# A gated cross-attention and mixture-of-experts kernel: first stage with two kv buffers, squares and the statistics of x on ScalarE, and the gate one block later

## What is computed

```python
kv = einsum('bhil,bhjl->bijhl', k, v)               # k = v = context, 8 x 8 products a head
y = irfft(rfft(kv, 2 * L) * rfft(ssm_kernel, 2 * L))[..., :L]
out = einsum('bijhl,bhil->bjhl', y + kv * D, q)     # q = layernorm(x)
x = x + tanh(g_xattn) * out
t = layernorm(x)
x = x + tanh(g_ffn) * (routed_experts(t) + shared_expert(t))
```

## Time and profile before

| | |
|---|---|
| median of three runs | 766.82 us (766.34 to 770.25) |
| the profiled execution | 769.46 us, span 767.5 us |
| PE busy | 725.1 us, 94% of the span |
| PEld busy | 675.8 us, 88% |
| DVE busy | 577.8 us, 75% |
| ACT busy | 431.1 us, 56% |
| POOL busy | 381.5 us, 50% |
| DMA | 114.32 MB, mean 149 GB/s |

### The profile page before, as it was taken

How to read it: one execution, slowest core, us unless ns; L and a number is a source line. 1 busy time by engine, 2 the same in 40 slices (tenths; PEclk the granted TensorE clock), 3 DMA queues, 4 the chain that set the end, 5 groups by cost and what they waited for, 6 DMA issues and landing times.

```text
span 767.5 us, 15537 instructions
## 1 busy us (share of the span) xinstructions
PE 725.1 (94%) x4602; PEld 675.8 (88%) x4602; DVE 577.8 (75%) x1152; ACT 431.1 (56%) x579; POOL 381.5 (50%) x191
## 2 busy tenths in 40 slices
PE   2899999999999999999999999999999999999993
PEld 2889899989888999999998999889899989999992
DVE  5889898999975469433799588679758985895892
ACT  3444444444432322123789577668758875895882
POOL 2898989888800137021335443344343435544242
PEclk9999999999999999999999999999999999999998
DMA  6658677776522211263466577677646575434200
GB/s 194 224 188 246 226 238 236 229 246 218 207 96 70 56 28 42 42 242 74 129 173 178 116 256 182 176 188 197 176 112 179 139 210 149 94 73 72 42 16 0
DMA packets 47425, 114.32 MB, mean 149 GB/s; under 512 B 7392, under 2 KB 7392, under 8 KB 47360
## 3 DMA queue, kind: packets, MB, share of 16 engines
q1 hardware_dynamic: 34528, 88.62, 34.8%
q0 software_dynamic: 12832, 24.93, 17.3%
HBM read 157.25 MB, written 29.26 MB: 243 GB/s over the span
## 4 chain that ended last, share of the span: by engine, by line
PE 58%; DVE 16%; DMA 8%; issue 7%; ACT 5%; SPq 2%; ACTq 1%; DVEq 1%; POOL 0%; POOLq 0%
PE pair L1196 15%; PE bank L1196 12%; PE pair L1221 10%; PE bank L1221 5%; PE pair L1132 5%; DMA out<-ys,slot_info 4%; DMA raw<-in_weights 3%; PE bank L1090 3%; PE bank L1143 3%; PE pair L1204 2%; DVE st L693 2%; DVE prod L746 2%; DVE bank L751 2%; DVE rows L758 2%; ACT xn L550 2%
## 5 line engine op out<-in xcount | busy, mean ns | idle before, releaser
L1063 DVE TENSOR_TENSOR w_lo<-raw,w_hi 128x1408 fp32r<-128x1408 f32 x94 | 148.8, 1622 | 44.8 <-ACT w_hi L650 44.8
L1319 POOL DMA_INDIRECT tn<-t_rows,slot_info x47 | 71.2, 1516 | 134.1 <-DVE tT_lo L803 117.6
L1330 POOL DMA_INDIRECT out<-ys,slot_info x47 | 86.3, 1836 | 100.3 <-DMA out<-ys,slot_info 70.6
L650 ACT ACTIVATE w_hi<-raw 128x1408 fp32r x94 | 124.9, 1375 | 5.9 <-DMA raw<-in_weights 3.8
L1132 PE MATMUL pair<-kv_hi,toep_hi 128*128 128x288 f32 x320 | 100.5, 314 | 4.4 <-issue 1.9
L1068 DVE TENSOR_TENSOR w_lo<-raw,w_hi 128x1536 fp32r<-128x1536 f32 x47 | 82.4, 1754 | 17.4 <-ACT w_hi L657 17.2
L1132 PE MATMUL pair<-kv_hi,toep_lo 128*128 128x288 f32 x320 | 95.3, 298 | 0.0
L1132 PE MATMUL pair<-kv_lo,toep_hi 128*128 128x288 f32 x320 | 95.1, 297 | 0.0
L1275 POOL TENSOR_TENSOR kv_lo<-kv,kv_hi 128x2304 fp32r<-128x2304 f32 (+1 forms) x16 | 79.6, 4972 | 18.8 <-ACT kv_hi L582 18.8
L657 ACT ACTIVATE w_hi<-raw 128x1536 fp32r x47 | 69.4, 1477 | 15.5 <-DMA raw<-in_weights 15.4
L1330 POOL DMA_INDIRECT out<-ys,own_row x16 | 27.4, 1713 | 82.5 <-ACT ys L638 76.1
(11 more groups left out here) (213 smaller groups left out, 2012.6 us busy)
## 6 DMA issues: line engine op xcount, KB each, us to landing
raw<-in_weights SPq DMA_DIRECT2D x94, 704.0 KB
raw<-in_weights SPq DMA_DIRECT2D x47, 768.0 KB
toep_hi<-kpad_hi SPq DMA_DIRECT2D x16, 512.0 KB, 4.1
toep_lo<-kpad_lo SPq DMA_DIRECT2D x16, 512.0 KB, 6.0
cx<-in_ctx SPq DMA_DIRECT2D x16, 384.0 KB, 6.3
stage<-in_weights SPq DMA_DIRECT2D x16, 272.0 KB, 4.5
xt<-in_x SPq DMA_DIRECT2D x16, 256.0 KB, 6.4
xr<-in_x SPq DMA_DIRECT2D x16, 256.0 KB, 6.5
```

The source lines that it names most:

```text
L650: act.activation(w_hi[s % 2][:, a:b], raw[:, bass.ds(half + a, b - a)], ACT.Copy).then_inc(hi_ok[n_], 1)
L1063: dve.tensor_tensor(w_lo[s % 2][:, a:b], raw[:, bass.ds(half + a, b - a)], w_hi[s % 2][:, a:b].bitcast(F32), ALU.subtract).then_inc(lo_ok[ ...
L1319: pool.indirect_dma_start(out=tn[o % 2][:], out_offset=None, in_=t_rows, in_offset=bass.IndirectOffsetOnAxis(ap=slot_info[:, 3 * i:3 * i + ...
L1330: pool.indirect_dma_start(out=out, out_offset=bass.IndirectOffsetOnAxis(ap=rows, axis=0), in_=ys[o % 2][:], in_offset=None, bounds_check=R ...
```

## The change

`kv` gets a second buffer. `form` leaves out the squares (3 groups of pairs in place of 4 in its first operation), and POOL does it for tile `t+2` in turn `t`, still ahead of `split_shared(t)` and `split_kv(t+1)`; `form(1)` goes ahead of the first turn. The squares are written by a new `square(t)` on ACT, also two tiles ahead; `split_kv_hi` waits for it. The mean and variance of `x` come from ACT: a Copy with scale -1/L and a Square with the negated mean as bias, both with `accum_out`, and the full outputs go to a scratch tile `spent`. DVE's `stats_x` goes, and `scale_x(t+1)` moves ahead of `products(t,2)`. In ACT's turn `split_shared`, `split_kv_hi` and `std_x` go ahead of `std_x2`. SP loads `ctx` one tile earlier. PE does `gate(t-2)` behind `conv(t,1)` in place of behind `conv(t,0)`.

```diff
--- before.py
+++ after.py
@@ -202,16 +202,17 @@
...
-        st1, st2 = sb2("st1_", [P, 6], F32, one), sb2("st2_", [P, 6], F32, one)
+        st2 = sb2("st2_", [P, 6], F32, one)
         mv1, mv2 = sb2("mv1_", [P, 3], F32, one), sb2("mv2_", [P, 3], F32, one)
         sd1, sd2 = sb2("sd1_", [P, 2], F32, one), sb2("sd2_", [P, 2], F32, one)
-        kv = sb("kv", [P, BLOCKS * GROUPS * PAIRS], F32, one)
+        kv = sb2("kv", [P, BLOCKS * GROUPS * PAIRS], F32, one)
...
+        spent = sb("spent", [P, L], F32, one)
...
@@ -271,7 +272,7 @@
...
-        q_turned, q_ok, kv_ok = sem("q_turned"), sem("q_ok"), sem("kv_ok")
+        q_turned, q_ok, kv_ok, square_ok = sem("q_turned"), sem("q_ok"), sem("kv_ok"), sem("square_ok")
...
@@ -302,11 +303,12 @@
...
-            n = (TILES - 4) // 2
+            n = (TILES - 6) // 2
...
-            turn(At(TILES - 1))
+            for t in range(TILES - 3, TILES):
+                turn(At(t))
@@ -362,16 +364,16 @@
         def form(eng, t):
 
             p = t.odd
-            wait(eng, kvl2_ok, t)
-            if t.within(1, 2):
+            wait(eng, kvl2_ok, t - 1)
+            if t.within(2, 3):
                 eng.wait_ge(kvl_ok, 1)
             wait(eng, ctx_in[p], (t.half() + 1) * 16)
             g, hb = BLOCKS * 2, HD * BATCH
-            eng.tensor_tensor(view(kv[:], 0, [[PAIRS * BATCH, g], [hb, 4], [1, hb]]),
-                              view(cx[p][:], 0, [[EXT * BATCH, g], [0, 4], [1, hb]]),
-                              view(cx[p][:], 0, [[EXT * BATCH, g], [BATCH, 4], [1, hb]]),
+            eng.tensor_tensor(view(kv[p][:], hb, [[PAIRS * BATCH, g], [hb, 3], [1, hb]]),
+                              view(cx[p][:], 0, [[EXT * BATCH, g], [0, 3], [1, hb]]),
+                              view(cx[p][:], BATCH, [[EXT * BATCH, g], [BATCH, 3], [1, hb]]),
                               ALU.mult).then_inc(kv_ok, 1)
-            eng.tensor_tensor(view(kv[:], 4 * hb, [[PAIRS * BATCH, g], [1, hb // 2]]),
+            eng.tensor_tensor(view(kv[p][:], 4 * hb, [[PAIRS * BATCH, g], [1, hb // 2]]),
                               view(cx[p][:], 0, [[EXT * BATCH, g], [1, hb // 2]]),
                               view(cx[p][:], hb // 2, [[EXT * BATCH, g], [1, hb // 2]]),
                               ALU.mult).then_inc(kv_ok, 1)
@@ -429,6 +431,9 @@
             load(At(0), "toep")
             load(At(1), "ctx")
             load(At(1), "x")
+            sp.wait_ge(kv_ok, 2)
+            sp.wait_ge(square_ok, 1)
+            load(At(2), "ctx")
             load(At(1), "toep")
             sp.dma_start(gw[:], gate_w).then_inc(consts_in, 16)
...
@@ -444,9 +449,11 @@
 
             def turn(t):
                 first, ahead = t.within(0, 1), not t.within(TILES - 2, TILES)
+                if not t.within(TILES - 3, TILES):
+                    wait(sp, kv_ok, (t + 2) * 2)
+                    wait(sp, square_ok, t + 2)
+                    load(t + 3, "ctx")
                 if ahead:
-                    wait(sp, kv_ok, (t + 1) * 2)
-                    load(t + 2, "ctx")
                     wait(sp, xn_ok, t + 1)
                     load(t + 2, "x")
                 if not first:
@@ -536,8 +543,17 @@
             act.activation(small[:, 3:4], small[:, 0:1], ACT.Sqrt)
 
             def std_x(t):
+
+                p = t.odd
+                wait(act, x_in[p], (t.half() + 1) * 16)
+                wait(act, rstd1, (t - 1) * 2)
+                act.activation(spent[:], xt[p][:], ACT.Copy, scale=-1.0 / L, accum_out=mv1[p][:, 0:1]).then_inc(stat1, 1)
+                wait(act, stat1, t * 2 + 1)
+                act.activation(spent[:], xt[p][:], ACT.Square, bias=mv1[p][:, 0:1],
+                               accum_out=mv1[p][:, 1:2]).then_inc(stat1, 1)
                 wait(act, stat1, (t + 1) * 2)
-                act.activation(sd1[t.odd][:, 0:1], mv1[t.odd][:, 1:2], ACT.Sqrt, bias=small[:, 0:1]).then_inc(std1, 1)
+                act.activation(sd1[p][:, 0:1], mv1[p][:, 1:2], ACT.Sqrt, bias=small[:, 0:1],
+                               scale=1.0 / L).then_inc(std1, 1)
 
...
@@ -579,7 +595,19 @@
                 p = t.odd
                 wait(act, conv_ok, (t - 1) * 8)
                 wait(act, kv_ok, (t + 1) * 2)
-                act.activation(kv_hi[p][:], kv[:], ACT.Copy).then_inc(kvh_ok, 1)
+                wait(act, square_ok, t + 1)
+                act.activation(kv_hi[p][:], kv[p][:], ACT.Copy).then_inc(kvh_ok, 1)
+
+            def square(t):
+
+                p = t.odd
+                wait(act, kvl2_ok, t - 1)
+                if t.within(2, 3):
+                    act.wait_ge(kvl_ok, 1)
+                wait(act, ctx_in[p], (t.half() + 1) * 16)
+                g, hb = BLOCKS * 2, HD * BATCH
+                act.activation(view(kv[p][:], 0, [[PAIRS * BATCH, g], [1, hb]]),
+                               view(cx[p][:], 0, [[EXT * BATCH, g], [1, hb]]), ACT.Square).then_inc(square_ok, 1)
 
...
@@ -587,26 +615,31 @@
                 wait(act, stage_in[p], (t.half() + 1) * 16)
                 act.activation(shared_hi[:, bass.ds(t.v * STAGE, STAGE)], stage[p][:], ACT.Copy).then_inc(shi_ok, 1)
 
+            square(At(0))
             act.wait_ge(kpad_ok, 1)
             act.activation(krow_hi[:], krow[:], ACT.Copy).then_inc(krowh_ok, 1)
             split_kv_hi(At(0))
             std_x(At(0))
             norm_x(At(0))
             q_copy(At(0))
+            square(At(1))
 
             def turn(t):
-                if not t.within(0, 1):
+                first, last = t.within(0, 1), t.within(TILES - 1, TILES)
+                split_shared(t)
+                if not last:
+                    split_kv_hi(t + 1)
+                    std_x(t + 1)
+                if not first:
                     std_x2(t - 1)
-                split_shared(t)
-                if not t.within(TILES - 1, TILES):
-                    split_kv_hi(t + 1)
-                if not t.within(0, 1):
+                if not t.within(TILES - 2, TILES):
+                    square(t + 2)
+                if not first:
                     norm_x2(t - 1)
-                if not t.within(TILES - 1, TILES):
-                    std_x(t + 1)
+                if not last:
                     norm_x(t + 1)
                     q_copy(t + 1)
-                if not t.within(0, 1):
+                if not first:
                     tT_copy(t - 1)
 
             pairs(act, turn)
@@ -695,18 +728,14 @@
                 dve.tensor_copy(hop[:, 1:2], hop[:, 0:1])
                 dve.bn_aggr(mv[p][:, 0:2], st[p][:]).then_inc(ok, 1)
 
-            def stats_x(t):
-                wait(dve, x_in[t.odd], (t.half() + 1) * 16)
-                stats(xt, st1, mv1, stat1, t)
-
             def scale_x(t):
 
                 p = t.odd
                 wait(dve, std1, t + 1)
                 dve.reciprocal(sd1[p][:, 1:2], sd1[p][:, 0:1]).then_inc(rstd1, 1)
                 wait(dve, rstd1, t * 2 + 1)
-                dve.tensor_scalar(mv1[p][:, 2:3], mv1[p][:, 0:1], sd1[p][:, 1:2], -1.0,
-                                  ALU.mult, ALU.mult).then_inc(rstd1, 1)
+                dve.tensor_scalar(mv1[p][:, 2:3], mv1[p][:, 0:1], sd1[p][:, 1:2], None,
+                                  ALU.mult).then_inc(rstd1, 1)
 
...
@@ -769,7 +798,6 @@
             form(dve, At(0))
-            stats_x(At(0))
             dve.memset(prod[0][:], 0.0).then_inc(setup_dve, 1)
             scale_x(At(0))
             dve.memset(prod[1][:], 0.0).then_inc(setup_dve, 1)
@@ -788,10 +816,8 @@
                 if not first:
                     scale_x2(t - 1)
                 if not last:
-                    stats_x(t + 1)
+                    scale_x(t + 1)
                 products(t, 2)
-                if not last:
-                    scale_x(t + 1)
                 products(t, 3)
 
             pairs(dve, turn)
@@ -1149,11 +1175,11 @@
             def turn(t):
                 first, last = t.within(0, 1), t.within(TILES - 1, TILES)
                 conv(t, 0)
-                if not first and not t.within(1, 2):
-                    gate(t - 2)
                 if not first:
                     sum_rows(t - 1, 3)
                 conv(t, 1)
+                if not first and not t.within(1, 2):
+                    gate(t - 2)
                 sum_rows(t, 0)
                 conv(t, 2)
                 sum_rows(t, 1)
@@ -1272,14 +1298,15 @@
 
                 wait(pool, kvh_ok, t + 1)
                 a = KV_DVE if t.within(0, 1) else 0
-                pool.tensor_tensor(kv_lo[t.odd][:, a:], kv[:, a:], kv_hi[t.odd][:, a:].bitcast(F32),
+                pool.tensor_tensor(kv_lo[t.odd][:, a:], kv[t.odd][:, a:], kv_hi[t.odd][:, a:].bitcast(F32),
                                    ALU.subtract).then_inc(kvl2_ok, 1)
 
             split_kv(At(0))
+            form(pool, At(1))
 
             def turn(t):
-                if not t.within(TILES - 1, TILES):
-                    form(pool, t + 1)
+                if not t.within(TILES - 2, TILES):
```

(3 more changed lines are left out.)

## The result

The changed kernel takes 760.64 us in the median of six runs (759.89 to 764.45); the kernel before, in six, 767.11 us. The ratio is 0.9905, 95% interval 0.9885 to 0.9925. Forecast were 759.7 us, 7.1 less; measured are 6.5 less in the medians, and the interval of the ratio spans 5.8 to 8.8. The profiled execution of the changed kernel took 759.89 us, its span is 758.1.

The account below looks back on a forecast made before the run. The prediction took a loop through four engines, 13.01 us a tile, to bound the first stage. Fourteen tiles save 9.8 us, the start costs 2.7, so 766.8 - 7.1 = 759.7 us; range 755 to 765.

Parts of the forecast that it names:

- The loop of four engines: First stage: `conv`, `products`, residual, `std_x2`, `kv_hi`, `kv_lo`, next `conv` take 13.01 us, the whole tile; cutting removes 0.36 a tile.
- Second buffer, form ahead: POOL, each tile: its ring goes, `form` takes 3.3 us, and POOL's 10.6 us a tile, at most 11.7, stay hidden.
- Statistics on ACT: ACT, each tile: Copy 0.65, Square 0.81, Sqrt 0.29 us, lower values taken; both statistics in time for DVE; ACT 8.1 us busy.
- The place of `scale_x`: DVE, ahead of `products(t,2)`: `xn` ready near +8.9 where PE asks at +11.3, removing the 0.38 us wait at `turn_q`.
- The gate: PE, behind `conv(t,1)`: path to `sum_rows(t,1)` keeps its length, gate done at about +4.2; nothing gained, nothing lost.
- step on ACT's order: ACT's turn: `q` and two copies end at about +1.1, `kv_hi` at +3.7; POOL's `kv_lo` ends at +8.9 instead of +12.8.
- What is late next: PE: `sum_rows(t,1)` still waits for `rows`, starting at +7.08; the new tile is 12.29 us against 13.01, 0.70 less taken.
- the first rival: First stage: all PE waits go, the tile is PE's own 11.97 us, 11.3 us less, 755.5 us; chance 0.12.
- The start: Before the steady tiles: four things come later, POOL's two `form`s longest; `conv(1,0)` at 32.4 instead of 29.71, +2.7 us.
- The path by DVE: Start of the first stage: from `shared_hi(0)` near 23.3 us through two `products`, 0.5 us shorter than POOL's path to `conv(1,0)`.
- The sum: Whole kernel: -9.8 us over fourteen tiles and +2.7 at the start give -7.1 us; the stage behind moves as a block.

Follow-up runs that it names:

- the run with all three edits: Changed kernel with `form` behind `split_kv`, the statistics of x2 behind `products(t,1)`, and `ctx(2)` loaded behind `stage(1)`: 753.8 us, ratio 0.9819.

## Why the prediction was right

*The loop of four engines*: right. Put back, together with the old place of `scale_x`, it gives 12.96, and the trace shows it closed; taken out alone, it gives 12.68.

*Second buffer, form ahead*: right as to the path, wrong by 0.2 in one size. `form` took 3.49, not 3.3; it was hidden by the same slack. So was a wait of `form` for `ctx`, 1.05 us in the tile shown, which the prediction did not have. Alone the buffer gives nothing. Whether it is needed at 12.24 no run shows: with the order of ACT alone POOL's ring on the single buffer took 12.5 to 12.6 us, but with 0.85 of that for the squares, and without them it would be an estimated 11.7.

*Statistics on ACT*: right, at the lower values that were taken and not in between the bounds. From the start of the Copy to the start of `std_x`'s Sqrt are 1.60 us (108.98 to 110.58), where 1.66 were taken; reading an accumulator is an instruction of its own, 0.19 to 0.21, and about covers the self-waits of 0.1 that I had put in. Behind the two at its start no table load stands in the first stage. The Trainium skill, "ScalarE: Activation LUTs", "Table sets: the hidden batching unit", says that cheap functions are in every set. The trace agrees in that Square ran beside Sqrt, Copy and Identity with no load, though the page does not list it there.

*The place of `scale_x`*: `xn` came in time, as said. The 0.44 us a tile were measured for this place and the statistics on ACT together, against 0.38 forecast; that the place matters more than DVE's shorter sum was argued and is not shown.

*The gate*: the step that failed, though its size did not spoil the sum. "Nothing gained" followed the gate's result and overlooked what the gate reads, `tT`, which ACT copies behind the two copies of `q`. First the kernel before, then the changed one:

```profile
107.64 0.61 ACT L575 ACTIVATE tT<-bank 128x512 f32<-128x512 f32 x1
108.40 0.97 PE L1111 MATMUL bank<-gw,tT 128*128 128x16 f32 x8
```

```profile
105.93 0.60 ACT L591 ACTIVATE tT<-bank 128x512 f32<-128x512 f32 x1
```

In the kernel before, `tT` was done 0.74 us behind the start of `conv` (107.51) and the gate began 0.15 later. In the changed kernel the copies come closer to `conv` and `tT` is done 1.15 behind it (105.38), so the old place would be too early. The prediction's own step on ACT's order had these copies end at about +1.1, and did not carry it over to the gate. The move is worth 0.10 us a tile.

*What is late next*: right in kind, 7.20 for 7.08. The 0.12 are the wait of `products` for `q`: the step took the 0.69 behind `conv` as fixed, and did not follow the path `turn_q`, `q_copy`, `products`, which ends 0.12 later. PE's tail was 1.34 for 1.43, and the tile 12.32 for 12.29. That the statistics of x2 stand in the way of PE's own pace was shown by moving them, with the 0.17 us of `logits_copy`: 11.91, where the first rival had 11.97.

*The start*: 1.90 for 2.7 at `conv(1,0)`. `form(1)` started at 16.77, not 17.5: `krow_hi` moved by 0.45, and `ctx(1)` landed no later than before. The path by DVE was off too, without effect on `conv(1,0)`: the first product came at 16.40 for 17.7, since `kv_lo(0)` started at 14.87 and took 1.43 for 2.56. The second half of the step was missing: PE's clock fell. With products at 0.24 in place of 0.133, `conv(1,0)` lasted 1.44 us where it lasts 0.88 in the steady tile, and tile 1 gained 0.39 of the 0.70. How much of the missing 0.31 is the clock is open: in the run with all three edits the clock stayed at 1.00, and tile 1 still took 12.24 against 11.92 later. The two errors are 0.8 and 0.3 us and of opposite sign. The order of POOL makes 1.05 of the 1.90, since `form` behind `split_kv` gives 30.56; the load of `ctx(2)` makes the rest, since with it moved as well `conv(1,0)` is at 29.68.

*The sum* at `conv(15,0)`: -8.0 for -7.1; 0.03 a tile and the start make the 0.9. That the medians, with -6.5, come as near to the forecast on the other side is luck in part: they contain the scatter of the second stage, which the forecast took to move as a block.

## What to carry to other kernels

When an engine waits without a name, follow the instruction that it needed back through the engines until the sum of the steps is the period. If it closes, as 13.01 did here, look for a cut by order before one by buffers; here the order alone helped and the buffer alone did not: 0.3 us of work that waited for another engine at the head of an in-order queue cost 0.29 us a tile. After the cut, look for the paths that end within 0.2 us of the new period; here these were `q` and `tT`, and each showed up in a trace. A queue that is filled further ahead pays for it once at the start, in front of the first piece that others wait for.

## What the runs showed of the hardware

The same operation of DVE, `kv_lo` of 128 x 1280, took 2.56 us in the kernel before and 1.43 in the changed one:

```profile
14.87 1.43 DVE L792 TENSOR_TENSOR kv_lo<-kv,kv_hi 128x1280 fp32r<-128x1280 f32 x1
```

```profile
12.13 2.35 POOL L1301 TENSOR_TENSOR kv_lo<-kv,kv_hi 128x1024 fp32r<-128x1024 f32 x1 [10.40 <-ACT kv_hi L599]
```

In the changed kernel POOL's part has ended at 14.48; in the kernel before DVE's began at 13.35 (rows 7), while POOL's ran. Of the ten kernels of the experiments three have it beside POOL's part, with 2.56 us (the buffer alone, the statistics on DVE, the order of ACT alone), and seven apart, with 1.43. The Trainium skill, "GPSIMD Engine Reference", "Specifications", says that POOL shares its SBUF interfaces with DVE and that DVE's instructions with two SBUF inputs contend; the trace agrees. DVE's operation took 1.13 us longer, nearly the 1.21 for which POOL's, done at 14.56, still ran beside it.

In the changed kernel the granted clock fell from 1.00 to 0.50 at about 31.8 us, behind idle spells of PE of 0.54, 0.62 and 1.04 us between 28.0 and 31.6. Idle time alone doesn't tell when it falls: one spell of 1.43 us in the kernel before, in front of the same products, left it at 1.00, and so did two of 1.35 and 1.86 us in the run with `std_x2` first:

```profile
28.00:30.00 2.00, 1.17 (x9) 0.96 (x9) 1.97 (x7) 1.19 (x3) 2.00 (x1) 1.00 1.01 315
30.00:32.00 2.00, 0.14 (x2) 0.16 (x2) 0.03 (x1) 0.37 (x2) 1.92 (x2) 1.00 0.94 171
32.00:34.00 2.00, 2.00 (x17) 2.00 (x18) 1.34 (x6) 0.00 (x0) 2.00 (x1) 1.00 1.01 376
```

Nor is the stretch at the lower level always as long. It ended at about 35.2 in the changed kernel. In the run with the statistics of x2 moved it lasted from about 30.3 to 37.2, with PE busy from 31.58 on, and tile 1 took 13.55 us there against 12.56. What decides either, no run here shows.
